# A mixture-of-experts stage: one expert's token rows are requested before its weights instead of after them

## Chip, cores and metric

The program runs on one core of a Trainium2 chip. The metric is the device time of one execution in microseconds (us), as the median of several executions. The engines are named as in the profile: PE (matrix multiplication), PEld (its weight loads), DVE, ACT, POOL, and SP, which computes nothing here and issues the DMAs.

## What is computed

A block with cross attention, self attention and a mixture of experts, each with a layer norm ahead and a residual behind it. The change lies in the third part, whose core is this:

```python
T = B * S                       # 512 tokens, D = 512
cap = max(1, int(T * 1.25 / E)) # E = 8 experts, cap = 80
probs_full = softmax(xt @ gate_w)
top_p, top_i = lax.top_k(probs_full, 2)
for k in range(2):
    ...                         # each token gets a place pos_c in expert e, if there is one left
    buf = zeros((E, cap, D)).at[e, pos_c].set(xt * keep)
    h = gelu(einsum('ecd,edf->ecf', buf, w1) + b1)     # 512 -> 2048
    y = einsum('ecf,efd->ecd', h, w2) + b2             # 2048 -> 512
    y = y + einsum('ecr,erd->ecd', gelu(einsum('ecd,edr->ecr', buf, wd)), wu)
    out = out + y[e, pos_c] * keep * top_p[:, k]
out = out + 0.2 * shared_expert(xt)
```

All is float32, and x is (2, 256, 512).

## The kernel before

Queries, cross attention and self attention take about the first 1650 us of the span; `experts` (from line 1355) takes the rest. In it the shared expert runs first, while the routing is worked out and POOL scatters the token rows into `buf_dram` in HBM (2 x 80 rows of 512 for each of 8 experts). Then the eight experts run one after the other, each over 160 row places.

**One expert on PE** (`expert`, L1904). First layer: eight groups `layer1(n)` of L1914 read the weights `w1[i]` and the transposed rows `bufT`, and write `h_ps`. After the fourth group `turn(e - 1)` (L1890) transposes the outputs of the expert before. After the fifth come eight short matmuls with `wd` (L1924). After the eighth, `fetch(e + 1, ...)` (L1883) transposes the rows of the **next** expert out of `xe`; it waits at L1875 until they have landed. Then the second layer reads `w2[i]`: four pieces, each of matmuls of L1937 and one of L1938 with `wu`. Its last matmul raises `y_ps`. PE works in program order, so a wait at `fetch` holds the second layer too. `w1`, `w2`, `wd`, `wu` and `xe` have two buffers each; i and q are the expert's number modulo 2.

**ACT** applies the gelu to each first layer group (L1754), copies the turned outputs (L1762) and the transposed rows (L1749). **DVE** adds the bias to the outputs (L1667), and during expert 7 adds the results of experts 0 to 6 to the residual (L1660), gathered by POOL from HBM (L1545).

**SP** issues every load. When expert e is finished on PE (`y_ps`, L1498), the buffers of that number modulo 2 are free, and SP asks for expert e + 2: four pieces of `w1` of 1 MB (L1460), `wd` (L1461), `wu` (L1462), four pieces of `w2` of 1 MB (L1466), and then the rows of e + 2 out of `buf_dram` (L1471, 320 KB). Then it waits until ACT has copied the outputs of expert e, and stores them (L1475). All of these go through one DMA queue. The loop runs for e = 0 to 5, so the rows of experts 2 to 7 come out of it. The rows of e + 2 are what `fetch` wants in expert e + 1. Experts 0 and 1 are loaded ahead of the loop (L1480 to L1493).

Of the kernel before, what the change touches and what calls it, by code (L numbers as in the profile page):

```python
# [1354 lines left out]
def experts(nc, a, out, buf_dram, y_dram, X, ident):  # L1355
# [24 lines left out]
    with ExitStack() as ctx:  # L1380
# [66 lines left out]
        @block.sync  # L1447
        def _(sp):
            sp.dma_start(gate[:, :, :], a["L0_ffn_gate_w"].rearrange("(c p) e -> p c e", p=P)).then_inc(s["gate_ld"], 16)
            for g in range(FC // PG):  # L1450
                w = slice(g * PG * P, (g + 1) * PG * P)
                sp.dma_start(w1[1][:, :, w], a["L0_ffn_sw1"][:, w].rearrange("(c p) n -> p c n", p=P)).then_inc(sw_ld[min(g, 2)], 16)
                sp.dma_start(w2[1][:, g * PG:(g + 1) * PG, :], a["L0_ffn_sw2"][w, :].rearrange("(c p) n -> p c n", p=P)).then_inc(sw_ld[min(g, 2)] if g else s["sad_ld"], 16)
                if g == 0:
                    sp.dma_start(wd[1][:, :, :], a["L0_ffn_swd"].rearrange("(c p) r -> p c r", p=P)).then_inc(s["sad_ld"], 16)
                    sp.dma_start(wu[1][:, :], a["L0_ffn_swu"]).then_inc(s["sad_ld"], 16)

            def expert_loads(e, i):
                for c in range(KC):
                    sp.dma_start(w1[i][:, c, :], a["L0_ffn_w1"][bass.ds(e, 1), c * P:(c + 1) * P, :].rearrange("o p n -> (o p) n")).then_inc(w1_ld[i], 16)  # L1460
                sp.dma_start(wd[i][:, :, :], a["L0_ffn_wd"][bass.ds(e, 1), :, :].rearrange("o (c p) r -> p (o c) r", p=P)).then_inc(ad_ld[i], 16)  # L1461
                sp.dma_start(wu[i][:, :], a["L0_ffn_wu"][bass.ds(e, 1), :, :].rearrange("o r n -> (o r) n")).then_inc(ad_ld[i], 16)  # L1462

            def expert_loads2(e, i):
                for c in range(4):
                    sp.dma_start(w2[i][:, c * 4:(c + 1) * 4, :],  # L1466
                                 a["L0_ffn_w2"][bass.ds(e, 1), c * 4 * P:(c + 1) * 4 * P, :].rearrange("o (c p) n -> p (o c) n", p=P)).then_inc(w2_ld[i], 16)

            def rows_load(e, q):

                sp.dma_start(xe[:, q, :, :], buf_dram[bass.ds(e, 1), :, :, :].rearrange("o k s d -> s (o k) d")).then_inc(s["xe_ld"], 16)  # L1471

            def rows_store(e, q):
                sp.wait_ge(s["yt_hi"], e * K + K)
                sp.dma_start(y_dram[bass.ds(e, 1), :, :, :].rearrange("o k s d -> s (o k) d"), y_rows[:, q, :, :]).then_inc(s["y_st"], 16)  # L1475

            sp.wait_ge(s["consts"], 1)
            for m in range(E // 2):
                sp.dma_start(buf_dram[2 * m:2 * m + 2, :, :, :].rearrange("e k s d -> s (e k) d"), xe[:, :, :, :].rearrange("s q k d -> s (q k) d")).then_inc(s["zeroed"], 16)
            expert_loads(0, 0)  # L1480

            sp.wait_ge(s["routed"], TT * K * 16)
            rows_load(0, 0)
            sp.wait_ge(s["sh_ps"], FC)
            expert_loads2(0, 0)
            sp.wait_ge(s["xe_ld"], 16)
            rows_load(1, 1)

            sp.wait_ge(s["s1_lo"], FC)
            sp.wait_ge(s["s2_lo"], FC)  # L1490
            sp.wait_ge(s["so_ps"], TT)
            expert_loads(1, 1)
            expert_loads2(1, 1)  # L1493
            with sp.Fori(0, (E - 2) // 2) as m:
                for q in range(2):
                    e = m * 2 + q

                    sp.wait_ge(s["y_ps"], e * 2 + 2)  # L1498
                    expert_loads(e + 2, q)
                    expert_loads2(e + 2, q)  # L1500
                    rows_load(e + 2, q)
                    rows_store(e, q)
            rows_store(E - 2, 0)
            for i in range(TT):

                sp.wait_ge(s["c_ok"], K * TT - TT + i + 1)
                sp.dma_start(out[i // RT, i % RT * P:(i % RT + 1) * P, :], X[:, i, :]).then_inc(s["stored"], 16)
            sp.wait_ge(s["stored"], TT * 16)
# [486 lines left out]
```

## Time and profile before

| what | us |
|---|---|
| median of 3 executions | 2147.81 (2147.12 to 2148.52) |
| the profiled execution | 2143.38 |
| its span in the trace | 2141.6 |
| PE busy in the span | 1981.4 |
| the eight experts on PE, from the first matmul of L1914 to the last of L1938 | 1747.67 to 2126.74 |
| PE held at `fetch`, six times together | 40.0 |

Times of the trace count from the start of the span. The profiled execution is 4.4 us shorter than the median of the unprofiled ones. PEclk is the granted clock of TensorE as a share of full speed (1.00 is 2.4 GHz, 0.50 is 1.2 GHz; values between are means over a stretch).

### The profile page before, as it was taken

The numbers are of one execution on the slowest core, as the hardware profiler recorded it, in microseconds if no ns is written. First come the engines' busy times: TensorE is split into PE (matmuls) and PEld (weight loads), VectorE is DVE, ScalarE is ACT, GpSimd is POOL, SyncE is SP. The second block draws the span as 40 slices with busy tenths as digits, with TensorE's granted clock in tenths as the row PEclk, the third lists the DMA queues.
The fourth block names the chain that finished last, engine by engine and source line by source line (L and its number), as shares of the span: only waits on it lengthen the run. The fifth ranks groups of instructions, "written<-read, shape, count | busy, mean of one in ns | idle before, by whom it ended". The sixth has DMA issues, their size and how long they took to land. (4 is left out here: it accounts for less than half of the span.)

```text
span 2141.6 us, 32804 instructions
## 1 busy us (share of the span) xinstructions
PE 1981.4 (93%) x10420; PEld 1637.6 (76%) x10420; DVE 1130.7 (53%) x2524; ACT 1036.6 (48%) x2356; POOL 314.7 (15%) x252
## 2 busy tenths in 40 slices
PE   7899999999999999999999999997888998888888
PEld 6687777877887778777877787775644888888887
DVE  3456666666766655766666666665675320000002
ACT  3202766676676760176676667667363431111111
POOL 0200111211111121011111121113142100000001
PEclk9899999999999999999999999999899999999998
DMA  7452111111111245311111111113005455444442
GB/s 226 160 172 78 36 44 41 47 34 42 42 34 39 69 148 194 101 37 43 43 34 43 41 47 34 34 40 107 12 0 185 157 196 220 172 172 171 171 172 61
DMA packets 127153, 198.11 MB, mean 93 GB/s; under 512 B 12461, under 2 KB 69989, under 8 KB 122976
## 3 DMA queue, kind: packets, MB, share of 16 engines
q1 hardware_dynamic: 123120, 188.59, 26.6%
q10 hardware_dynamic: 2672, 4.55, 0.6%
q0 software_dynamic: 1280, 3.93, 0.5%
q8 instruction: 46, 0.75, 0.1%
q14 instruction: 35, 0.29, 0.0%
HBM read 151.50 MB, written 45.81 MB: 92 GB/s over the span
## 5 line engine op out<-in xcount | busy, mean ns | idle before, releaser
L698 DVE TENSOR_TENSOR crs_ptl<-crs_tp,crs_pth 128x512 fp32r<-128x512 f32 x512 | 352.2, 690 | 225.9 <-ACT crs_pth L566 224.3
L566 ACT ACTIVATE crs_pth<-crs_tp 128x512 fp32r<-128x512 f32 x512 | 305.8, 597 | 209.7 <-PE crs_tp L910 209.7
L495 POOL TENSOR_TENSOR crs_vl<-crs_vraw,crs_vh 128x512 fp32r<-128x512 f32 x128 | 165.0, 1289 | 1116.1 <-ACT crs_vh L573 1116.1
L901 PE MATMUL crs_ring<-crs_kh,crs_ql 128*128 128x512 f32 x512 | 234.6, 458 | 3.9 <-DVE crs_ql L738 3.9
L920 PE MATMUL crs_ov<-crs_ptl,crs_vh 128*128 128x512 f32 x512 | 208.6, 407 | 19.0 <-DVE crs_ptl L698 19.0
L910 PE MATMUL crs_tp<-all_ident,crs_prob 128*128 128x128 f32 x1024 | 197.4, 274 | 26.7 <-ACT crs_more L560 26.7
L910 PEld LDWEIGHTS crs_tp<-all_ident,crs_prob 128*128 128x128 f32 x1024 | 138.8, 140 | 101.7 <-ACT crs_more L560 44.3
L901 PE MATMUL crs_ring<-crs_kh,crs_qh 128*128 128x512 f32 x512 | 202.3, 395 | 0.0
L920 PE MATMUL crs_ov<-crs_pth,crs_vh 128*128 128x512 f32 x512 | 202.2, 395 | 0.0
L901 PE MATMUL crs_ring<-crs_kl,crs_qh 128*128 128x512 f32 x512 | 201.2, 393 | 0.0
L920 PE MATMUL crs_ov<-crs_pth,crs_vl 128*128 128x512 f32 x512 | 200.3, 391 | 0.0
L910 PE MATMUL crs_tp<-all_ident,crs_more 128*128 128x128 f32 x1024 | 195.6, 273 | 0.0
L560 ACT ACTIVATE crs_prob<-crs_prob,crs_nmax 128x512 f32<-128x512 f32 x256 | 183.9, 718 | 14.4 <-DVE crs_nmax L713 14.4
L1667 DVE TENSOR_SCALAR ex_yT<-moe_bank,moe_b_cols 128x160 f32<-128x160 f32 x32 | 10.8, 379 | 337.3 <-PE moe_bank L1938 337.3
L560 ACT ACTIVATE crs_more<-crs_more,crs_nmax 128x512 f32<-128x512 f32 x256 | 183.6, 717 | 0.0
L577 ACT ACTIVATE crs_kh<-crs_ring 128x512 fp32r<-128x512 f32 x128 | 76.6, 598 | 214.7 <-PE crs_ring L890 212.5
L708 DVE CUSTOM_DVE_ANT_0 crs_prob<-crs_ring,crs_maskb 128x512 f32<-128x512 f32 x256 | 172.7, 683 | 3.4 <-PE crs_ring L901 3.3
L708 DVE CUSTOM_DVE_ANT_0 crs_more<-crs_ring,crs_maskb 128x512 f32<-128x512 f32 x256 | 172.9, 683 | 0.8 <-PE crs_ring L901 0.8
L1754 ACT ACTIVATE ex_hT<-moe_bank,moe_b_cols 128x160 f32<-128x160 f32 x128 | 43.6, 391 | 255.8 <-PE moe_bank L1914 254.3
L702 DVE TENSOR_TENSOR crs_kl<-crs_ring,crs_kh 128x512 fp32r<-128x512 f32 x128 | 88.6, 692 | 146.7 <-ACT crs_kh L577 146.7
L1914 PE MATMUL moe_bank<-moe_bufT,moe_w 128*128 128x160 f32 x1024 | 146.0, 302 | 0.7 <-ACT moe_bufT L1749 0.7
L1914 PEld LDWEIGHTS moe_bank<-moe_bufT,moe_w 128*128 128x128 f32 x1024 | 141.2, 192 | 4.0 <-issue 2.2
(269 smaller groups left out, 3533.9 us busy)
## 6 DMA issues: line engine op xcount, KB each, us to landing
moe_w<-in_L_ffn_w SPq DMA_DIRECT2D x48, 1024.0 KB, 12.3
v_scratch<-crs_more SPq DMA_DIRECT2D x64, 512.0 KB, 2.9
crs_vraw<-v_scratch SPq DMA_DIRECT2D x128, 256.0 KB, 2.7
ex_w<-in_L_ffn_w SPq DMA_DIRECT2D x16, 1024.0 KB, 13.4
crs_prob<-in_ctx SPq DMA_DIRECT2D x32, 256.0 KB, 3.8
crs_wo<-in_L_xattn_Wo SPq DMA_DIRECT2D x16, 512.0 KB, 4.1
moe_w<-in_L_ffn_sw SPq DMA_DIRECT2D x8, 1024.0 KB, 12.8
qry_wq<-in_L_xattn_Wq SPq DMA_DIRECT2D x16, 256.0 KB, 4.0
```

The costliest lines, as they stand in the source:

```text
L495: nc.gpsimd.tensor_tensor(vl[:, n % VR, :, :], vraw[:, :, :], vh[:, n % VR, :, :].bitcast(F32), ALU.subtract).then_inc(s["v_lo"], 1)
L560: act.activation(w, w, ACT.Exp, bias=nmax[:, t:t + 1], accum_out=rs[:, t, n:n + 1]).then_inc(s["p_ready"], 1)
L566: act.activation(pth[:, k % PT, :], tp[k % PT][:, :], ACT.Copy).then_inc(s["pt_hi"], 1)
L577: act.activation(kh[:, n % KR, :], ring[k_at(n, op) % RING][:, :], ACT.Copy).then_inc(s["keys_hi"], 1)
L698: v.tensor_tensor(ptl[:, k % PT, :], tp[k % PT][:, :], pth[:, k % PT, :].bitcast(F32), ALU.subtract).then_inc(s["pt_lo"], 1)
L702: v.tensor_tensor(kl[:, n % KR, :], ring[k_at(n, op) % RING][:, :], kh[:, n % KR, :].bitcast(F32), ALU.subtract).then_inc(s["ring_free"], 1)
L708: v.tensor_tensor_reduce(probs(t, n * BANK, (n + 1) * BANK), ring[at % RING][:, :], maskb[:, n * BANK:(n + 1) * BANK], op0=ALU.add, op1=AL ...
L901: m = pe.matmul(ring[at % RING][:, :], a[:, t // RT, rows], w[:, n % KR, :], start=i == 0, stop=i == 2)
L910: m = pe.transpose(tp[k % PT][:, t * P:(t + 1) * P], probs(t, k * P, (k + 1) * P), ident[:, :])
L920: m = pe.matmul(ov[:, :], a[:, k // NC % VR, k % NC, :], w[:, k % PT, :], start=k == 0 and i == 0, stop=k == SCH - 1 and i == 2)
L1754: m = act.activation(hT[:, 2 * n + q, :], h_ps[n % 2][:, q * SL:(q + 1) * SL], ACT.Gelu, bias=b1_cols[:, bass.ds(e * FC + (2 * n + q), 1)])
L1914: m = pe.matmul(h_ps[n % 2][:, q * SL:(q + 1) * SL], w1[i][:, c, fc * P:(fc + 1) * P], bufT[:, i, c, :], start=c == 0, stop=c == KC - 1)
```

## The change

In SP's loop the call that loads the rows stands first. Nothing else is touched, and the other engines' programs are the same.

```diff
                     sp.wait_ge(s["y_ps"], e * 2 + 2)
+                    rows_load(e + 2, q)
                     expert_loads(e + 2, q)
                     expert_loads2(e + 2, q)
-                    rows_load(e + 2, q)
                     rows_store(e, q)
```

On SP, at the head of the loop body (e even), right behind the wait for `y_ps`; `moe_xe` are the rows, `moe_w1_0` is the first layer's weight buffer 0, and an ISA row is the register work or wait ahead of a DMA:

```order
@@ -190,4 +190,6 @@
 L1494 UNCONDITIONAL_BRANCH
 L1494 ISA
+L1471 ISA
+L1471 DMA moe_xe<-buf_scratch 80x2x512
 L1460 ISA
 L1460 DMA moe_w1_0<-in_L0_ffn_w1 128x2048
```

The rows' DMA now stands ahead of the first piece of `w1`.

Further down in the same loop body on SP, where the loads of an even expert end and those of the odd one begin (`ex_w2_0` is the second layer's weight buffer 0, `y_scratch<-ex_y_rows` the store, L1498 the wait for `y_ps` of the odd expert):

```order
@@ -202,9 +204,9 @@
 L1462 DMA moe_wu_0<-in_L0_ffn_wu 32x512
 L1466 DMA ex_w2_0<-in_L0_ffn_w2 128x4x512 x4
-L1471 ISA
-L1471 DMA moe_xe<-buf_scratch 80x2x512
 L1475 ISA
 L1475 DMA y_scratch<-ex_y_rows 80x2x512
 L1498 ISA
+L1471 ISA
+L1471 DMA moe_xe<-buf_scratch 80x2x512
 L1460 ISA
 L1460 DMA moe_w1_1<-in_L0_ffn_w1 128x2048
```

The rows' DMA has moved from between `w2` and the store to the head of the list, ahead of ten weight DMAs; the store now follows `w2` directly.

## Rows read from the trace of the kernel before

**Rows 1.** The page, part 1: busy us, share of the span, instructions.

```profile
PE   1981.4 (93%) x10420; PEld 1637.6 (76%) x10420; DVE 1130.7 (53%) x2524; ACT 1036.6 (48%) x2356; POOL 314.7 (15%) x252
```

**Rows 2.** Waits, PE, 1740 to 2142 us: us in total, times, longest us.

```profile
PE moe_bank L1883 <- DMA moe_xe<-buf_scratch: 40.0, 6, 7.3
```

**Rows 3.** Windows of experts 0, 1 and 7: stretch, length, busy by engine.

```profile
core 0: us, PE busy (x) PEld busy (x) DVE busy (x) ACT busy (x) POOL busy (x), PEclk, DMA share, GB/s
1747.60:1789.30 41.70, 41.32 (x282) 39.27 (x283) 0.84 (x3) 6.39 (x19) 0.00 (x0) 0.96 0.65 238
1789.30:1839.90 50.60, 43.42 (x289) 41.20 (x289) 1.18 (x4) 7.57 (x21) 0.00 (x0) 0.90 0.49 182
...
2085.90:2126.80 40.90, 39.90 (x280) 37.65 (x280) 7.65 (x15) 6.69 (x19) 11.60 (x9) 1.00 0.19 54
```

**Rows 4.** The chain that ended last, 1788 to 2127 us: start, us, what.

```profile
1788.63 0.48 PE moe_bank L1938 x2
1789.29 0.35 SPq L1460
...
1800.61 2.48 SPq L1466
1803.28 12.82 DMA moe_xe<-buf_scratch
1816.14 1.33 PE moe_bank L1883 x8
1817.46 6.84 PE moe_bank L1937 x32
...
2014.84 5.46 PE moe_bank L1937 x32
...
2085.87 8.89 PE moe_bank L1914 x64
...
2105.73 0.92 issue
2106.65 4.58 PE moe_bank L1937 x32
...
2126.26 0.48 PE moe_bank L1938 x2
```

**Rows 5.** Timeline around `fetch` in experts 0 and 1, and DVE in 7: start, us.

```profile
1767.99 0.72 PE L1883 MATMUL moe_bank<-all_ident,moe_xe 80*128 80x80 f32 x8
1768.20 0.68 ACT L1754 ACTIVATE ex_hT<-moe_bank,moe_b_cols 128x160 f32<-128x160 f32 x2 [1.49 <-PE moe_bank L1914]
1769.02 4.58 PE L1937 MATMUL moe_bank<-ex_hT,ex_w 128*128 128x160 f32 x32 [0.30 <-ACT ex_hT L1754]
...
1802.17 6.79 PE L1914 MATMUL moe_bank<-moe_bufT,moe_w 128*128 128x160 f32 x48
...
2112.70 5.51 DVE L1660 SCALAR_TENSOR_TENSOR all_X<-moe_w,moe_topp,all_X 128x512 f32<-128x512 f32 x8 [26.00 <-DMA moe_w<-y_scratch,moe_idx]
```

**Rows 6.** Short windows in experts 3 and 7, columns as in Rows 3.

```profile
1901.00:1905.00 4.00, 4.00 (x30) 3.62 (x29) 0.00 (x0) 1.40 (x5) 0.00 (x0) 1.00 1.06 377
...
1913.00:1916.00 3.00, 0.00 (x0) 0.00 (x0) 0.00 (x0) 0.00 (x0) 0.00 (x0) 0.50 0.48 139
1916.00:1920.00 4.00, 3.94 (x19) 3.95 (x20) 0.00 (x0) 0.88 (x2) 0.00 (x0) 0.50 0.00 2
...
2103.00:2107.00 4.00, 3.08 (x23) 2.86 (x22) 0.00 (x0) 1.36 (x4) 3.09 (x4) 1.00 0.61 175
```

**Rows 7.** DMA issues, 1683 to 1737 us: expert 0's rows with nothing beside them.

```profile
moe_xe<-buf_scratch SPq DMA_DIRECT2D x1, 320.0 KB, 3.0
```

**Rows 8.** Line L1471 (rows), 1786 to 2095 us, six DMAs: issue, then landing.

```profile
L1471 SPq DMA_DIRECT2D moe_xe<-buf_scratch x6: 2077/2608/3027, 1803.3 to 2049.8; - x6
...
DMA to landing us min/median/max: 12.7/13.1/14.1
```

**Rows 9.** Line L1460 (`w1`), 1786 to 2095 us, 24 DMAs: landing.

```profile
DMA to landing us min/median/max: 4.9/7.8/12.3
```

**Rows 10.** Line L1466 (`w2`), 1786 to 2095 us, 24 DMAs: landing.

```profile
DMA to landing us min/median/max: 11.8/14.0/16.1
```

## The prediction, made before the changed kernel ran

> **What bounds the kernel now.** I read the busy shares first. PE is busy for 93% of the span [rows 1], so it is the engine whose idle time counts. The question is whether the change meets any of the remaining 7%. The waits of the expert stage answer it: PE stood at L1883, the transposes of `fetch`, six times for 40.0 us together, 7.3 at most, and each time for the rows `moe_xe` [rows 2]. Six is the number of experts whose rows come out of SP's loop (2 to 7). No other wait of PE in the eight experts is as long as 1 us; the longest is the 0.92 us between the layers of expert 7 [rows 4].
>
> The chain of waits shows what makes the rows late. The last matmul of expert 0 ends at 1788.63 + 0.48 = 1789.11. SP issues its first weight DMA at 1789.29 and its last at 1800.61, which takes 2.48 us. Only then come the rows, at 1803.28, and they take 12.82 us. PE begins the transposes at 1816.14 [rows 4]. It had finished its first layer at 1802.17 + 6.79 = 1808.96 [rows 5], so it lost 7.2 us. The rows are 320 KB and with nothing beside them they land in 3.0 us [rows 7]; in the loop they need 12.7 to 14.1 us [rows 8]. At that time the DMA engines are busy throughout (share 1.06, 377 GB/s) [rows 6], with up to 8 MB of weights asked for before. The rows stand in line behind weights that nobody wants for a long while yet.
>
> The second effect is PE's clock. While PE stands, the granted clock falls to 0.50 (1.2 GHz) and it is still 0.50 in the 4 us after work resumes [rows 6]. The first piece of the second layer takes 6.84 us in expert 1 and 5.46 in the best of the six, against 4.58 in expert 7, where PE had not stood at `fetch` [rows 4].
>
> **The part removed: the wait of six experts.** The cleanest measure of an expert without this wait is expert 7, which has no `fetch`. It lasts from 2085.87 to 2126.26 + 0.48 = 2126.74, that is 40.87 us [rows 4], at a granted clock of 1.00 [rows 3]. It does have the `turn` of the expert before, as experts 1 to 6 have. What it lacks are the eight transposes. What do they cost when the rows are there? Expert 0 shows it: they take 0.72 us, from 1767.99 to 1768.71, while ACT still works on the last gelu until 1768.88, and PE goes on at 1769.02 because of ACT, not because of them [rows 5]. So they lie wholly beside a wait that expert 7 has too (0.92 us) [rows 4], and I count them at nothing. If that cover were gone they would cost 6 x 0.72 = 4.3 us.
>
> Experts 1 to 6 now last from 1789.11 to 2085.87, that is 296.76 us [rows 4]. Without the wait they should last 6 x 40.87 = 245.22. The difference is **51.5 us**. A check by parts: 40.0 of waiting [rows 2]; transposes at the low clock, 6 x 1.33 = 8.0; the slow first pieces, between 6 x (5.46 - 4.58) = 5.3 and 6 x (6.84 - 4.58) = 13.6; less the gap of 6 x 0.92 = 5.5 that stays [rows 4]. That is 47.8 to 56.1, and 51.5 lies in the middle.
>
> Are the rows really in time? PE wants them 19.9 us after SP's start signal (2105.73 - 2085.87) [rows 4]. The request goes out 0.2 us after it (1789.29 against 1789.11) [rows 4]. Nothing is in the queue then but, at most, the store of an earlier expert, asked for right behind the last rows at 1803.28 [rows 4] and so most of a period before. So the nearest row is the load alone, 3.0 us [rows 7], and I take landing at about 3.2. The other end is the slowest rows load of the loop, 14.1 us [rows 8], as if the weights asked for later all pushed in beside it: 14.3 us. Both ends are before 19.9, so the whole range of this unknown costs nothing, and the wait goes entirely and not in part.
>
> **The part moved: ten weight DMAs start later.** The rows' issue costs SP 2.1 to 3.0 us when the queue is full [rows 8]. In an empty queue it should be nearer to the 0.35 us that the first weight DMA takes [rows 4]; 0.35 is my value, 3.0 the bound. The four pieces of `w1` come first, at 0.35 us an issue [rows 4] with the register work between them, so the last is out by about +2 (an estimate), and it lands at most 12.3 us later [rows 9]: at +14.3, with the bound of 3.0 at +17.3. PE wants it when expert e + 1 is done, now at +40.9. That leaves 23 us. The last `w2` is issued at 1803.1, +14.0 [rows 4], and lands at most 16.1 later [rows 10]: +30.1, or +33.1. It is wanted at 40.9 + 19.9 = +60.8. The cover thus holds with the shorter period. In sum the stage needs about 30 us of transfers in each 40.9, where it had 49.5. The store (L1475) leaves SP a little earlier than before, and the wait ahead of it holds nothing but itself.
>
> **What is late next.** Behind `fetch` PE waits for `w2` of e + 1, asked for one period earlier, and for the last gelu, which is the 0.92 us already counted. The end of the kernel also hangs on DVE: the results of experts 0 to 6 are added from 2112.70 to 2118.21 [rows 5], and DVE must be free at 2126.74. This chain starts from the outputs of expert 6, so it shifts with PE, and its slack of 8.5 us stays. Nothing in stages ahead of the loop is touched.
>
> **The sum.** On the profiled execution's own time: 2143.38 - 51.5 = 2091.9. On the median: 2147.81 - 51.5 = **2096.3 us**. The 4.4 us between the two cannot be placed from the trace. If they lie in these same waits the gain is 4.4 larger, 2091.9. On the other side, if an expert with transfers beside it lasted as long as the window of expert 0 (41.70 us) [rows 3] and not 40.87, the gain would be 6 x 0.83 = 5.0 smaller, 2101.3. Expert 0's length has causes of its own (a mean clock of 0.96 [rows 3]), so I stay with 40.87.
>
> **Rivals.**
>
> *The clock falls all the same.* The wait goes, but the short pause between the layers lets the granted clock drop, and the second layer starts slowly as now. Then the first pieces keep their 6.84 to 5.46 us (between 5.3 and 13.6 us, about 9.4, not gained), and the transposes at 1.33 us outlast the 0.92 gap by 6 x 0.41 = 2.5: 2096.3 + 9.4 + 2.5 = 2108. Against it: in expert 7 the window with that pause has PE busy for 3.08 of 4 us and the clock at 1.00 [rows 6]. The Trainium skill (TensorE: Matmul & The Clock Gate, section A second HAM failure mode: psum-queue depth-cycling) says that short idle stretches between groups of matmuls can be enough to make the clock swing. By that rule the time would be this rival's; the trace here does not agree, since the clock stayed at 1.00 over a pause of 0.92 us. Chance 3%.
>
> *The change doesn't do what it says.* The DMA engines might not serve the queue in the order of issue, so that the rows land only with all the weights asked for after them, at about +27 as now. Then nothing changes: 2147.8. Against it: the `w1` pieces, asked for first, land in 4.9 us at the least and the later `w2` pieces in 11.8 to 16.1 [rows 9, 10], which is the picture of a line in order. Chance 2%.
>
> *The weights become the bound, and the kernel is slower.* With 40.9 us instead of 49.5 between two signals, `w1` of e + 2 could be missing when its expert starts, and rows in small packets ahead of it would push it back. It decides when `w1` lands later than +40.9, against at most +17.3 above; slower than now it is beyond +49.5. If each expert took 54 us, twice the 27 us from signal to landed rows now (1789.11 to 1816.1 [rows 4]), the kernel would be at 2147.8 + 6 x (54 - 49.5) = 2175. In expert 0, with transfers beside it for 0.65 of the time at 238 GB/s, PE was busy for 41.32 of 41.70 us [rows 3], so the transfers do not hold PE by their mere presence either. Chance 1%.
>
> *Only part of the gain.* The rows land late by something no row shows (a slower read of `buf_dram` beside the weights' first pieces). To leave half of the wait they would have to land near +23, 9 us beyond the slowest load seen. The time would be about 2096.3 + 20 to 26, some 2120. Chance 2%.
>
> **How the numbers follow.** Forecast 92%, at 2096.3; the four rivals have 8% together. The forecast's own spread, 2091.9 to 2101.3, with a little for the scatter of medians (1.4 us between the three runs before), gives 2090 to 2103 as the range for 8 in 10; it leaves out all rivals, which are under 2 in 10. A difference of 0.2% (4.3 us) is about what a measurement of this kernel can tell from no change. Faster by more than that: the forecast, the clock rival and the partial one, 97%. Within it: 2%. Slower: 1%.
>
> **What the profile afterwards should show.** The wait of PE at L1883 for `moe_xe` is gone from the list, or below 1 us in total. The rows land about 3 us after their issue, at +3 to +4; a landing over 14 would break my bound. Experts 1 to 6 last 40.9 us each, with a granted clock of 1.00, and the first L1937 piece takes 4.5 to 4.6 us in all. The chain of waits goes through PE alone from expert 0 to 7, without SPq or DMA pieces. `w1` and `w2` land by about +15 and +31. The prediction is wrong if PE shows a wait for `moe_w` or `ex_w` ahead of L1914 or L1937, if the clock sags in the second layers without a wait, or if the last part of the kernel, after 2126.74 before, becomes longer by itself.

## The result, and the profile after

The changed kernel takes 2096.16 us in the median (2093.95 to 2097.64, 4 executions) against 2147.49 us before (4 executions; a fourth, of 2147.18 us, has joined the three of the table). The ratio is 0.9759, with a 95% interval of 0.9742 to 0.9776: 51 us or 2.4% faster. The profiled execution took 2097.40 us with a span of 2095.7.

First the page of the kernel after. Beside [rows 1], PE is busy for about the same time in a shorter span:

```profile
span 2095.7 us, 32804 instructions
PE 1972.9 (94%) x10420; PEld 1629.4 (78%) x10420; DVE 1130.9 (54%) x2524; ACT 1034.9 (49%) x2356; POOL 314.5 (15%) x252
```

PE's waits from 1740 us to the end answer to [rows 2] (columns: us in total, times, longest). These are the four longest:

```profile
PE moe_bank L1937 <- ACT ex_hT L1754: 1.9, 5, 0.4
PE moe_bank L1901 <- DVE ex_yl L1646: 1.6, 1, 1.6
PE moe_bank L1937 <- issue: 1.3, 3, 0.8
PE moe_bank L1890 <- DVE ex_yT L1667: 0.8, 1, 0.8
```

The 40.0 us at L1883 for `moe_xe` are gone, and nothing of size stands in their place. The 1.6 and the 0.8 us stood in the list before, too; the two waits at L1937, ahead of the second layer, are the short pause between the layers, now in every expert. The windows of experts 0, 1, 2 and 7 answer to [rows 3], with the same columns:

```profile
1752.50:1795.40 42.90, 42.57 (x281) 40.51 (x281) 0.68 (x2) 6.37 (x19) 0.00 (x0) 0.93 0.62 229
1795.40:1836.10 40.70, 40.44 (x289) 38.34 (x289) 1.35 (x4) 7.33 (x21) 0.00 (x0) 1.00 0.61 227
1836.10:1877.00 40.90, 40.51 (x290) 38.40 (x289) 1.35 (x4) 7.33 (x21) 0.00 (x0) 1.00 0.60 225
...
2040.50:2081.20 40.70, 39.88 (x280) 37.67 (x280) 7.62 (x14) 6.68 (x19) 11.58 (x9) 1.00 0.20 55
```

Expert 1 lasted 50.6 us at a mean granted clock of 0.90 and now lasts 40.7 at 1.00. The DMA engines are busy for 0.61 of the time instead of 0.49: the same bytes in a shorter period. The chain that ended last, beside [rows 4] (start, us, what):

```profile
1752.53 13.99 PE moe_bank L1914 x80
...
1795.37 8.89 PE moe_bank L1914 x64
1804.26 0.87 PE moe_bank L1890 x8
1805.14 2.17 PE moe_bank L1914 x16
1807.31 1.21 PE moe_bank L1924 x8
1808.52 6.72 PE moe_bank L1914 x48
1815.23 0.56 PE moe_bank L1883 x8
1816.05 4.58 PE moe_bank L1937 x32
...
2040.48 8.89 PE moe_bank L1914 x64
```

The chain is PE's own work from expert to expert. SP and the DMA of the rows no longer stand in it, and the first piece of the second layer takes 4.58 us where it took 6.84. The rows' DMAs themselves, line L1471, answer to [rows 8]:

```profile
L1471 SPq DMA_DIRECT2D moe_xe<-buf_scratch x6: 333/338/353, 1795.6 to 1999.9; - x6
DMA to landing us min/median/max: 3.2/3.5/3.5
```

Issue takes 0.34 us instead of 2.6, and landing 3.5 instead of 13.1. The landings of `w1` and of `w2` (L1460, then L1466), beside [rows 9, 10], are these:

```profile
DMA to landing us min/median/max: 5.2/8.9/13.0
DMA to landing us min/median/max: 11.7/14.1/16.8
```

For `w2` they have hardly moved. For `w1` the median is 8.9 us instead of 7.8, with the rows now ahead of it.

Where did the 45.9 us between the two spans come from? Each line below but the last is the difference of two starts in the two chains; the last runs to the end of the span:

| stretch | before, us | after, us | difference |
|---|---|---|---|
| up to the first L1914 of expert 0 | 1747.67 | 1752.53 | +4.86 |
| expert 0 | 41.44 | 42.84 | +1.40 |
| experts 1 to 6 | 296.76 | 245.11 | -51.65 |
| expert 7 and the end | 55.73 | 55.22 | -0.51 |

Expert 0 is longer by its first 80 matmuls: 13.99 us, where they took 12.56, at a mean granted clock of 0.93 over the expert instead of 0.96.

### The profile page after: what moved, and what is told of

Read it like the earlier page. It is cut to its first block and busy times, and to the rows that moved or that the text cites. A ratio compares the mean times of both kernels' runs of the same rounds, so it can differ in the third digit from the quotient of the medians.

```text
span 2095.7 us, 32804 instructions
## 1 busy us (share of the span) xinstructions
PE 1972.9 (94%) x10420; PEld 1629.4 (78%) x10420; DVE 1130.9 (54%) x2524; ACT 1034.9 (49%) x2356; POOL 314.5 (15%) x252
## 5 line engine op out<-in xcount | busy, mean ns | idle before, releaser
L1914 PE MATMUL moe_bank<-moe_bufT,moe_w 128*128 128x160 f32 x1024 | 147.4, 304 | 0.6 <-ACT moe_bufT L1749 0.6
L1914 PEld LDWEIGHTS moe_bank<-moe_bufT,moe_w 128*128 128x128 f32 x1024 | 142.6, 193 | 4.0 <-issue 2.2
```

Source lines behind the costliest of these rows:

```text
L1914: m = pe.matmul(h_ps[n % 2][:, q * SL:(q + 1) * SL], w1[i][:, c, fc * P:(fc + 1) * P], bufT[:, i, c, :], start=c == 0, stop=c == KC - 1)
```

## The experiments

Two theories had to be told apart. Mine: the rows were late because of their **place in the queue**, which is served in the order of issue; PE wants them 19.9 us after SP's signal, all that comes earlier is worth nothing more, and the weights have room. The rivals: only an empty queue helps; or the weights are close to being the bound; or the slow first piece has nothing to do with the clock. Ratios are to the kernel before on the same chip, where its median was 2146.45, 2149.26 or 2146.68 us; so times from different chips are compared by their ratios.

### Other places in the queue

Rows between `w1` and `w2` (against the changed kernel):

```diff
+                    expert_loads(e + 2, q)
                     rows_load(e + 2, q)
-                    expert_loads(e + 2, q)
                     expert_loads2(e + 2, q)
```

> The rows are asked for between w1 and w2. Theory (one queue, served in the order of issue, and PE wants the rows 19.9 us after SP's start signal): 4.1 MB stand ahead, which at the rate of the full queue (about 0.35 to 0.38 MB per us) are in by +14, so the rows land at +14 to +16 and there is no wait; the whole gain, 2094 to 2098 us. Rival (only an empty queue helps, and rows in the middle are served together with everything asked for after them): landing at +27, time as before, 2147.

Measured: 2096.31 us, ratio 0.9765 (0.9749 to 0.9782). The landings of the rows:

```profile
L1471 SPq DMA_DIRECT2D moe_xe<-buf_scratch x6: 327/331/349, 1800.7 to 2005.0; - x6
DMA to landing us min/median/max: 11.2/12.1/13.2
```

Expert 1 starts at 1797.00 there, so the rows are in at about 1800.7 + 12.1, or +15.8. That is four times as late as in the changed kernel, and the time is the same. Between these two places, then, it makes no difference how long before +19.9 the rows land.

Rows behind the first two, and behind the first three pieces of `w2`; the loads of `w2` are cut in two for that (against the kernel before):

```diff
                     expert_loads(e + 2, q)
-                    expert_loads2(e + 2, q)
+                    expert_loads2(e + 2, q, 0, 2)      # or 0, 3
                     rows_load(e + 2, q)
+                    expert_loads2(e + 2, q, 2, 4)      # or 3, 4
```

> The rows stand behind w1 and the first two pieces of w2, 6.2 MB, ahead of the last two. Theory (order of issue): landing at +20 to +21.5, against a need at +19.9, so PE waits 0.3 to 1.5 us per expert. A wait that short should leave the granted clock at 1.00: 2097 to 2106 us. Rival (any wait at this place brings the low clock with it): 1.5 us per expert more, 2110 to 2116.

> One more piece of w2 stands ahead, 7.2 MB. Theory: landing at +23 to +24, a wait of 3 to 4 us per expert; with the clock held 2117 to 2122 us, with the low clock afterwards up to 2132. Rival (together with everything asked for later): 2147.

Measured: 2109.85 us (0.9831, 0.9814 to 0.9847) behind two pieces and 2132.78 us (0.9946, 0.9928 to 0.9963) behind three. PE's wait, of the first and then of the second kernel:

```profile
PE moe_bank L1884 <- DMA moe_xe<-buf_scratch: 10.0, 6, 2.6
```

```profile
PE moe_bank L1884 <- DMA moe_xe<-buf_scratch: 26.8, 6, 5.8
```

Spread over six experts that is 1.7 and 4.5 us, beside 6.7 before [rows 2] and none in the kernel with the rows in the middle. With the need at +19.9 the mean landings are +21.6, +24.4 and +26.6, with six, seven and eight pieces of 1 MB ahead: each further piece costs 2.2 to 2.8 us. The order-of-issue picture holds. Both waits came out a little above my figures (0.3 to 1.5 and 3 to 4 us), since the landings were 0.1 to 0.4 us beyond the ends I gave. Both times missed their ranges: the second is just above its own (up to 2132), and the first, 2109.85, lies above the 2097 to 2106 of the theory and next to the 2110 to 2116 of the rival, by which any wait at this place brings the low clock with it. What failed is the sentence that so short a wait leaves the clock alone. The traces say in how many experts; see The clock's part.

### Half of the change

Against the kernel before:

```diff
+                    if q == 0:
+                        rows_load(e + 2, q)
                     expert_loads(e + 2, q)
                     expert_loads2(e + 2, q)
-                    rows_load(e + 2, q)
+                    if q == 1:
+                        rows_load(e + 2, q)
```

> Only the rows of the even experts (2, 4, 6) are asked for first, those of 3, 5 and 7 stay last. If each expert's gain is its own, it is half of the whole: 2147.5 - 25.7 = 2122 us, with three waits of 6 to 7.3 us left in the trace. If the gain of one expert only shifted the wait to the next (the weights being the bound), nearly nothing: above 2140.

Measured: 2121.99 us, ratio 0.9887 (0.9870 to 0.9903). The time is the 2122 expected, but the chip was another one; by the ratio the gain is 24 us (21 to 28), where half of the whole is 25.7.

```profile
PE moe_bank L1886 <- DMA moe_xe<-buf_scratch: 19.4, 3, 7.0
```

Three waits remain, of 6.5 us in the mean. Each expert's gain is its own, within about 1.5 us in all; nothing of size is handed on to the next.

### The same request through another queue

ACT asks for the rows, behind its copies of the turned outputs; the call in SP's loop is gone (against the changed kernel):

```diff
                 if not first:
                     turned(e - 1, 1 - q)
+                    if not last:
+                        act.dma_start(xe[:, 1 - q, :, :], buf_dram[bass.ds(e + 1, 1), :, :, :].rearrange("o k s d -> s (o k) d")).then_inc(s["xe_ld"], 16)
```

> The rows of the next expert are asked for by ACT, in its own DMA queue, behind its copies of the turned outputs, about 11 us after the expert's start, while SP's queue is full of weights. Theory (the place in the own queue decides, and two queues share the DMA engines): landing 3 to 6 us after the issue, +14 to +17, no wait: 2094 to 2098 us. Rival (the DMA engines' backlog counts, whatever the queue): landing 12 to 16 us after the issue, at +23 to +27, 2120 to 2147 us.

Measured: 2096.60 us, ratio 0.9764 (0.9748 to 0.9781). The request in expert 1 goes out at 1800.89, 9.8 us after the expert's start at 1791.08, and the six landings are these:

```profile
L1769 ACTq DMA_DIRECT2D moe_xe<-buf_scratch x6: 325/332/343, 1800.9 to 2005.3; - x6
DMA to landing us min/median/max: 7.7/7.9/8.1
```

Beside the backlog of SP's queue, but not in it, the 320 KB take 7.9 us: more than the 3.5 us of an empty queue and more than the 3 to 6 I expected, and less than the 13.1 behind the weights. It ends at about +17.7, 2 us before the need, so the full gain is there. So it was the place in the own queue that made the rows late, and not alone the load on the DMA engines. That place costs twice. In the kernel before SP comes to the request only at 1803.28, +14.2, having spent most of the time until then on issuing `w2` (one of these issues takes 6.82 us); the landing takes 12.8 us more. The first half of the delay is SP held by its full queue, and ACT is free of that as well. The Trainium skill (DMA: Bandwidth & Descriptors, section Queues, rings and completion order) says that each DMA engine takes turns between the queues that have work for it. The trace agrees, in that the rows did not have to wait for what was in SP's queue: 7.9 us against 13.1. In what shares the two queues were served is not shown.

### The clock's part

The loads stand as before, and PE fills its wait with 20 multiplications whose result nobody reads (against the kernel before):

```diff
                 if not last:
+                    if not first:
+                        for _ in range(20):
+                            pe.matmul(bank[7][:, 0:SL], w1[i][:, 0, 0:P], bufT[:, i, 0, :], start=True, stop=True)
                     fetch(e + 1, 1 - i, first)
```

> The order of the loads is that of before, but in experts 1 to 6 PE multiplies 20 times into an unused bank between the first layer and the transposes of the next rows, about 5.4 us of work whose result nobody reads. Theory (the pause lowers the granted clock, and that is what makes the transposes 1.33 instead of 0.72 us and the first piece of the second layer 5.5 to 6.8 instead of 4.58): the wait that is left is 0.3 to 2 us, the clock stays at 1.00, and each expert is 2.1 us shorter: 2133 to 2137 us. Rival (the slow piece comes from the transfers or from the waiting itself, and not from the clock): 2147.

Measured: 2135.42 us, ratio 0.9945 (0.9927 to 0.9963), 12 us by the ratio. The chain around the transposes in experts 1, 2 and 3 (start, us, what):

```profile
1820.45 0.77 PE moe_bank L1883 x8
...
1868.44 1.09 PE moe_bank L1883 x8
1869.53 5.74 PE moe_bank L1940 x32
...
1917.42 0.77 PE moe_bank L1883 x8
1918.19 4.39 PE moe_bank L1940 x32
```

The rows take as long to land as before (12.9 us in the median), and yet the kernel is faster, by doing more. In five of six experts the first piece takes 4.39 us. In expert 2, where the longest remaining wait (2.0 us) fell, it takes 5.74. The six first pieces together take 27.7 us instead of 36.7, and the transposes 4.9 instead of 7.9: 12.0 us, as much as by the ratio. So the slow work behind the wait is the clock's, and it is worth nearly a quarter of the gain (12 of 51 us). The rest of it, 39 us, is the waiting itself.

The kernel with the rows behind two pieces of `w2` says more on this. In its experts PE paused 2.40, 1.81, 2.62, 0.80, 0.53 and 1.85 us ahead of the transposes. Behind the four longer pauses the first piece took 6.06 to 6.07 us, behind the two short ones 4.39. So the rival of that kernel holds in four of its six experts. PE resumes at 1814.87 in expert 1 and at 1946.65 in expert 4; the windows after that (columns as in Rows 3):

```profile
1814.00:1816.00 2.00, 1.13 (x12) 1.14 (x13) 0.00 (x0) 0.60 (x2) 0.00 (x0) 0.99 1.04 384
1816.00:1818.00 2.00, 2.00 (x10) 2.00 (x9) 0.00 (x0) 0.16 (x1) 0.00 (x0) 0.50 1.04 388
...
1948.00:1950.00 2.00, 2.00 (x17) 2.00 (x16) 0.00 (x0) 0.00 (x0) 0.00 (x0) 1.00 1.04 384
```

The granted clock is 0.50 (1.2 GHz) behind the pause of 2.40 us and 1.00 behind the one of 0.80. In expert 1 it fell only once PE was at work again: the window with the transposes shows 0.99, and they took 0.77 us there, as in expert 4. In the kernel before, with pauses of 5.7 us and more, it had fallen while PE stood, and the transposes took 1.33.

### How much room the weights have

Rows first, then the store, which holds SP until ACT has copied the outputs, and `w1` last of all (against the kernel before):

```diff
-                    expert_loads(e + 2, q)
-                    expert_loads2(e + 2, q)
                     rows_load(e + 2, q)
                     rows_store(e, q)
+                    expert_loads2(e + 2, q)
+                    expert_loads(e + 2, q)
```

> Rows first, then the store, which holds SP until about +10.6, then w2, and w1 last. Theory (the weights have slack): all are in 26 us later, w1 at +37, and PE wants it at +40.9. No wait: 2094 to 2099 us. Rival (the weights are about to become the bound, the forecast's slack is wrong): waits of PE at L1914 for moe_w, above 2105.

Measured: 2095.76 us, ratio 0.9762 (0.9746 to 0.9778). SP's issues in expert 1, which starts at 1791.72 (start, us, ...):

```profile
1791.91 0.35 SPq L1471 DMA_DIRECT2D moe_xe<-buf_scratch  x1
1802.45 0.35 SPq L1475 DMA_DIRECT2D y_scratch<-ex_y_rows  x1
1803.00 3.47 SPq L1466 DMA_DIRECT2D ex_w<-in_L_ffn_w  x4
1806.57 5.52 SPq L1460 DMA_DIRECT2D moe_w<-in_L_ffn_w  x4
```

The landings of `w1` in that expert:

```profile
DMA to landing us min/median/max: 13.5/15.2/17.5
```

The last `w1` is issued before 1812.09 and lands at most 17.5 us later, at about +37.9; PE wants it at +40.8. Even so, no time is lost.

One step further, SP also waits until the next rows' transposes are done (beside the kernel just shown):

```diff
                     rows_load(e + 2, q)
                     rows_store(e, q)
+                    sp.wait_ge(s["g_ps"], e * 2 + 6)
                     expert_loads2(e + 2, q)
                     expert_loads(e + 2, q)
```

> As the kernel with w1 last, but SP waits further until the next rows' transposes are done (about +20.6) before it asks for any weights. Theory: w1 lands at +46 to +47, PE waits at the start of each of experts 2 to 7 for 5 to 6 us and works at the low clock afterwards, 1 to 2 us more: 48 to 49 us an expert, 2138 to 2147. It shows from where the weights decide.

Measured: 2139.36 us, ratio 0.9961 (0.9950 to 0.9972). The wait, and the chain at the start of expert 2:

```profile
PE moe_bank L1915 <- DMA moe_w<-in_L_ffn_w: 29.6, 6, 6.4
```

```profile
1820.87 18.39 DMA moe_w<-in_L_ffn_w
1839.26 0.24 issue
1839.50 11.54 PE moe_bank L1915 x64
```

Expert 1 starts at 1793.49, so `w1` is in at +45.8, and PE pays for it at the start of an expert: five microseconds of waiting and 11.54 instead of 8.89 us for the first 64 matmuls. This is the mechanism of the prediction's slower rival, made real, though not its size: the kernel is 43 us slower than the changed one by the medians, but still no slower than the kernel before. For the wait to come, `w1` had to land beyond +40.8; in the changed kernel it is in by about +16 at the latest (SP's last issue of it ends at +3.0, and the slowest landing takes 13.0 us).

### What was left: the pause between the layers

The changed kernel again, and beside it the same with one wait split. PE waits for seven of the eight groups of hidden rows, and for the last one only ahead of the two matmuls that read it (against the changed kernel):

```diff
-                pe.wait_ge(s["h_ok"], e * (FC // 2) + FC // 2)
+                pe.wait_ge(s["h_ok"], e * (FC // 2) + FC // 2 - 1)
                 for c in range(KC):
...
                     for n in range(FC):
+                        if c == 0 and n == FC - 2:
+                            pe.wait_ge(s["h_ok"], e * (FC // 2) + FC // 2)
```

> The changed kernel once more, beside the next one: 2094 to 2098 us.

> The changed kernel, and the second layer starts before the last gelu: PE waits for seven of the eight groups of hidden rows, and for the eighth only ahead of the last two of 16 matmuls of the first piece. The pause of 0.8 us between the layers then holds only the transposes, 0.56 to 0.72 us in experts 0 to 6, and nothing in expert 7: 0.1 to 0.3 us gained in each of seven and 0.8 in the last, 1.5 to 3 us in all, 2092 to 2095 against 2096. Rival: the pause has another cause, and nothing is gained.

Measured: 2094.91 us (2092.96 to 2097.40) and 2088.70 us (2087.81 to 2093.01); the ratios to before are 0.9757 (0.9743 to 0.9771) and 0.9736 (0.9720 to 0.9751). The second is 6.2 us below the first and below my range of 2092 to 2095. The intervals overlap a little, so the traces must carry it. Expert 2 of the kernel with the split wait:

```profile
1831.27 8.89 PE moe_bank L1914 x64
...
1844.41 6.72 PE moe_bank L1914 x48
1851.13 0.56 PE moe_bank L1883 x8
1851.68 4.39 PE moe_bank L1939 x32
...
1871.56 0.47 PE moe_bank L1914 x2
```

The second layer starts directly behind the transposes. Expert 2 lasts 40.29 us instead of 40.91 (1836.12 to 1877.03), experts 1 to 6 together 241.78 instead of 245.11, and expert 7, from 2032.75 to 2072.46, 39.71 instead of 40.77. That is 4.4 us in experts 1 to 7, more than the 1.5 to 3 in all that I expected: I had counted only the pause behind the transposes, at 0.1 to 0.3 us. It is 0.26 us in experts 1 and 6 and 0.39 in experts 2 to 5, and the first piece also takes 4.39 us instead of 4.58 to 4.61 when PE did not stand directly ahead of it. The other 1.8 us between the medians are not placed; they are no more than the scatter of the executions. This version is faster than both kernels of the study.

## Why the prediction was right

**The bound.** PE's wait at `fetch` for rows behind ten weight DMAs: right. It is gone from the list, and the kernels with other places bring it back in order: 0, 1.7, 4.5 and 6.7 us an expert.

**The sum.** Experts 1 to 6 were to last 245.22 us and last 245.11. The transposes cost next to nothing: they take 0.56 us of a pause of 0.82 in expert 1 and of 0.93 in expert 2. Expert 7 was thus the right yardstick, though its first piece has the small delay of 4.58 against 4.39 us in it, like the others'. That the sum agrees to 0.1 us is luck: experts 2 to 5 last 40.90 to 40.91 us each, and the yardstick itself took 40.87 us before and 40.77 after. That the median, 2096.16, lies 0.1 us from the 2096.3 forecast is luck too, since the four executions span 3.7 us.

**The clock.** It stays at 1.00. The first piece takes 4.58 to 4.61 us. The clock's part was rightly counted into the gain, and filling the wait gave it by itself, 12 us. The check by parts left the slow first pieces at 5.3 to 13.6 us; the six of the profile before are 9.2 us above 4.58 each, and with that the parts add up to 40.0 + 8.0 + 9.2 - 5.5 = 51.7. The rival by which the clock would fall over the pause between the layers did not come: the windows of experts 1 to 7 show 1.00. The margin was smaller than I thought, though: the kernel with the rows behind two pieces of `w2` shows the low clock behind a pause of only 1.81 us, and the pause that stays between the layers is 0.8 to 0.9.

**The landing.** Forecast +3.2, measured 0.2 + 3.5 = +3.7. The bound of 14.3 was never needed, but the rows at +15.8 show that even beyond it nothing is lost.

**The weights.** `w1` lands about 1 us later after its issue in the median, `w2` as before, and the slack of about 23 us for `w1` was confirmed from both sides: no loss with `w1` at +37.9, a loss with it at +45.8. The "about 30 us of transfers" in each expert was too high: it is the time of the last landing. By the windows the DMA engines are busy for 0.61 of 40.7 us, which is 24.8.

**The base.** On the profiled execution's own time I had 2091.9, and the profiled execution after took 2097.4. The 5.5 us are not in the experts of the loop. They are 4.86 us ahead of expert 0, where no instruction was changed, and 1.40 us in expert 0, less 0.5 us in expert 7 and behind it. In the twelve traces of this study expert 0 starts between 1747.67 (the profile before) and 1754.17 us, whatever the kernel. The profile before had the earliest start of all. In the four kernels with the full gain (the changed one, rows in the middle, ACT's queue, `w1` last) the profiled times differ by 5.9 us, and the time from the start of expert 0 to the end by 1.2. So the 4.4 us that I could not place were most likely those of an early profile, and not of longer waits in the other executions. There is no trace of those others, so this is argued and not shown. The prediction could not tell the two apart, and took the median because that is the metric.

## What to carry to other kernels

When a small transfer is late, look at what stands ahead of it in its own queue and at when each of those is wanted; move the small early one ahead of the large late ones, or into another queue. It is enough to beat the moment of need: the four kernels that did took 2095.76 to 2096.60 us. Count the slow clock behind a wait with the wait itself, and take the length without both from a stretch of the same profile that has neither.

## What was not expected of the hardware

- A pause as short as 1.81 us was followed by the low clock (first piece 6.06 us against 4.39), while pauses of 0.53, 0.80 and 1.33 us were not. Behind a pause of 2.40 us the clock was still at 0.99 when PE resumed, and 0.50 in the 2 us after. Another pause, of 2.0 us, went with 5.74 us. I had worked out the low clock only behind waits of 5.7 us and more.
- The same 320 KB landed in 3.5 us at the head of an empty queue, 7.9 in a second queue beside a full one, 12.1 behind four pieces of `w1` in the same queue, and 13.1 as the last request behind 8 MB, which SP could send only 14.2 us after the start signal.
- With nothing changed ahead of it, expert 0 started over a range of 6.5 us from trace to trace, and its first 80 matmuls took 12.50 to 14.12 us. The two traces of the changed kernel, though, agree to 0.1 us in this start. What sets it was not tried.
